# Group norm and attention over 16 images: the next image brought in as 16 pieces of four rows in place of 4 pieces of sixteen

## What is computed

```python
def _gn(v, G=32, eps=1e-5):
    ...
    m = jnp.mean(g, axis=(1, 2, 4), keepdims=True)
    s = jnp.var(g, axis=(1, 2, 4), keepdims=True)
    return ((g - m) / jnp.sqrt(s + eps)).reshape(v.shape)
...
qkv = jnp.einsum('bglc,dc->bgld', x, W_qkv) + b_qkv
score = jnp.einsum('bghlc,bghmc->bghlm', q, k) / scale
score = jax.nn.softmax(score, axis=-1)
out = jnp.einsum('bghlm,bghmc->bghlc', score, v)
...
x = x + _L0_conv_ref(_gn(x), L0_conv_W_qkv, L0_conv_b_qkv)
```

## Time and profile before

| what | value |
|---|---|
| median of 3 runs | 4365.6 us (4364.17 to 4367.62) |
| the profiled execution | 4368.04 us |
| its span in the profile | 4365.9 us |
| busy: PE, DVE, ACT, POOL | 3961.3, 3673.0, 3037.9, 1781.8 us |
| mean granted clock of PE | 0.963 of full speed |
| read from HBM, written | 134.42 MB, 134.22 MB |
| loads of images on ACT | 60 of 2048 KB, 9.6 us each to landing |
| DMA transposes on SP | 2048, 3.2 to 3.3 us each to landing |

### The profile page before, as it was taken

How to read it: one execution, slowest core, us unless ns; L and a number is a source line. 1 busy time by engine, 2 the same in 40 slices (tenths; PEclk the granted TensorE clock), 3 DMA queues, 4 the chain that set the end, 5 groups by cost and what they waited for, 6 DMA issues and landing times.

```text
span 4365.9 us, 144522 instructions
## 1 busy us (share of the span) xinstructions
PE 3961.3 (91%) x44133; PEld 3009.3 (69%) x44133; DVE 3673.0 (84%) x7138; ACT 3037.9 (70%) x8193; POOL 1781.8 (41%) x2065
## 2 busy tenths in 40 slices
PE   4898989989899898998989989899898988989998
PEld 3676767667676676766767667676676766767776
DVE  6896978879788797987979879798797987979987
ACT  3676767667676676766767667677676766767776
POOL 1443434434344343443434434344343433434444
PEclk9999999999999999999999999999999999999999
DMA  7999999999999999999999999999999999999999
GB/s 190 221 206 241 210 227 220 187 241 210 227 219 189 241 210 231 216 189 240 209 234 216 185 243 210 229 216 190 245 210 231 220 194 235 209 242 210 202 209 196
DMA packets 2508947, 944.11 MB, mean 216 GB/s; under 512 B 2180544, under 2 KB 2443072, under 8 KB 2508608
## 3 DMA queue, kind: packets, MB, share of 16 engines
q1 hardware_dynamic: 2384768, 814.22, 90.3%
q10 hardware_dynamic: 123840, 125.83, 9.1%
HBM read 134.42 MB, written 134.22 MB: 62 GB/s over the span
## 4 chain that ended last, share of the span: by engine, by line
PE 55%; DMA 13%; issue 12%; DVE 9%; SPq 7%; POOL 1%; ACT 1%; DVEq 1%; POOLq 0%; ACTq 0%
PE s_bank L297 15%; PE qk_bank L275 15%; PE o_bank L313 12%; DMA pt_hi<-p_hi 12%; PE v_bank L285 7%; PE xt_bank L267 4%; DVE neg_max L427 3%; SPq L227 3%; SPq L231 3%; PE v_bank L282 2%; DVE v_lo L440 1%; POOL p_hi L598 1%; DVE o_norm L453 1%; DVE bn L458 1%; DMA pt_lo<-p_lo 1%
## 5 line engine op out<-in xcount | busy, mean ns | idle before, releaser
L607 POOL TENSOR_TENSOR y_ring<-image,o_norm 128x256 f32<-128x256 f32 x1024 | 742.6, 725 | 2268.0 <-DVE o_norm L453 2268.0
L392 ACT ACTIVATE prob<-s_bank,neg_max 128x256 f32<-128x256 f32 x4096 | 1612.7, 492 | 69.8 <-issue 60.8
L373 ACT ACTIVATE qk<-qk_bank,b_in 128x256 f32<-128x256 f32 x2048 | 859.1, 471 | 950.8 <-PE qk_bank L275 949.5
L427 DVE TENSOR_REDUCE neg_max<-s_bank 128x2 f32<-128x512 f32 x2048 | 1313.2, 684 | 63.8 <-PE s_bank L297 62.8
L297 PE MATMUL s_bank<-qk 64*128 64x256 f32 x8192 | 1221.2, 418 | 45.5 <-issue 44.7
L434 DVE SCALAR_TENSOR_TENSOR p_lo<-prob,p_hi 128x1024 f16<-128x1024 f32 x1024 | 1239.5, 1210 | 4.9 <-POOL p_hi L598 1.4
L598 POOL TENSOR_SCALAR p_hi<-prob 128x1024 f16<-128x1024 f32 x1024 | 1068.6, 1044 | 312.4 <-DMA pt_hi<-p_hi 238.7
L275 PE MATMUL qk_bank<-xc,w_norm 128*128 128x256 f32 x4096 | 1190.1, 414 | 0.0
L313 PE MATMUL o_bank<-v_hi,pt_lo 128*128 128x65 f16 x8192 | 868.2, 195 | 282.0 <-DMA pt_hi<-p_hi 226.3
L275 PEld LDWEIGHTS qk_bank<-xc,w_norm 128*128 128x128 f32 x4096 | 714.1, 194 | 413.6 <-issue 342.9
L313 PEld LDWEIGHTS o_bank<-v_hi,pt_lo 128*128 128x128 f16 x8192 | 767.3, 99 | 304.1 <-DMA pt_hi<-p_hi 235.4
(11 more groups left out here) (71 smaller groups left out, 1922.8 us busy)
## 6 DMA issues: line engine op xcount, KB each, us to landing
x_ring<-image SPq DMA_DIRECT2D x512, 256.0 KB, 2.6
out_dram<-y_ring SPq DMA_DIRECT2D x512, 256.0 KB, 2.4
image<-in_x_dram ACTq DMA_DIRECT2D x60, 2048.0 KB, 9.6
pt_hi<-p_hi SPq DMA_TRANSPOSE x1024, 3.3
pt_lo<-p_lo SPq DMA_TRANSPOSE x1024, 3.2
image<-in_x_dram SPq DMA_DIRECT2D x4, 2048.0 KB, 16.5
w_in<-in_L_conv_W_qkv_dram SPq DMA_DIRECT2D x1, 192.0 KB, 2.4
b_in<-in_L_conv_b_qkv_dram SPq DMA_DIRECT2D x3, 0.5 KB, 2.1
```

The source lines that it names most:

```text
L373: ins = act.activation(qk[:, v % 2, t, :], qk_bank[:, t * TOK:(t + 1) * TOK], ACT.Identity, bias=b_in[:, t:t + 1])
L392: ins = act.activation(prob[:, m, c:c + TOK], s_bank[m][h][:, a * TOK:(a + 1) * TOK], ACT.Exp, bias=neg_max[:, m, h, a:a + 1])
L427: dve.tensor_reduce(neg_max[:, m, h, :], s_bank[m][h][:, :].rearrange("p (a k) -> p a k", a=J), AX.X, ALU.max, negate=True).then_inc(max_d ...
L607: pool.tensor_tensor(y_ring[:, m, :], image[:, par, bass.ds(row, 1), :].rearrange("p a c -> p (a c)"), o_norm[:, v % 2, :, :].rearrange("p ...
```

## The change

It has four parts. The next image but one is now brought in behind the image in work: in step r of image n, at every fourth step, ACT issues the load of four rows (r-20 to r-17) of image n+2 into the places of the same rows of image n, or, in steps 0 to 19, rows 44 to 63 of image n+1 into the places of image n-1. Each of the 15 images that are loaded so comes in 16 pieces of 512 KB, 240 loads in place of 60. The wait of each is for `y_done` to have passed the rows that it overwrites, 16 steps back. In image 0 the first 11 pieces of image 1 are issued within steps 0 to 7 with no wait. And the loop over images has 6 rounds in place of 7: images 13, 14 and 15 are written out, because the last two bring nothing or less.

```diff
-    LOADS = 4
...
-    SETTLE = UNROLL
-    assert SETTLE + LOADS * UNROLL <= STATS_FROM
+    LAG = STATS_FROM
+    CHUNKS = ROWS // UNROLL
...
+                if coming is not None and u == 0 and bring is not None:
+                    bring(base, *coming)
                 order(run, next_image)
...
                     for i in range(-2 * UNROLL, start):
-                        step(i // UNROLL * UNROLL, i // UNROLL * UNROLL, i % UNROLL, par, None,
-                             (LOAD, img + 1, 0) if i == UNROLL else None)
+                        if bring is not None and i >= 0:
+                            for c in range(i, CHUNKS - LAG // UNROLL, start):
+                                bring(None, 1, 1, c * UNROLL)
+                        step(i // UNROLL * UNROLL, i // UNROLL * UNROLL, i % UNROLL, par, None, None,
+                             (1, 1, ROWS - LAG + i) if i >= 0 else None)
...
                 with eng.Fori(0, GROUPS // UNROLL) as t:
                     for u in range(UNROLL):
                         step(t * UNROLL + g + STATS_FROM, t * UNROLL + STATS_FROM, u, par, None,
-                             None if last else (MEASURE, img + 1, t * UNROLL + u))
+                             None if last else (MEASURE, img + 1, t * UNROLL + u),
+                             None if final else (img + 2, par, t * UNROLL + (STATS_FROM - LAG)))
...
-            with eng.Fori(0, IMAGES // 2 - 1) as q:
+            with eng.Fori(0, IMAGES // 2 - 2) as q:
                 for s in range(2):
                     run_image(q * 2 + (1 + s), 1 - s, False, False)
-            run_image(IMAGES - 1, (IMAGES - 1) % 2, False, True)
+            for img in range(IMAGES - 3, IMAGES):
+                run_image(img, img % 2, False, img == IMAGES - 1)
...
-                if what[0] == LOAD:
-                    part = what[2]
-                    if not isinstance(what[1], int) or what[1] > 1:
-                        act.wait_ge(y_done, (what[1] - 1) * ROWS)
-                    rows = bass.ds(part * LB, LB)
-                    act.dma_start(image[:, 1 - par, rows, :], x_img[what[1], :, rows, :]).then_inc(loaded[1 - par], 16)
...
+            def bring(base, img, par, row, free=False):
+                if not (free or base is None or known_below(base, LAG)):
+                    act.wait_ge(y_done, base - (LAG - UNROLL))
+                rows = bass.ds(row, UNROLL)
+                act.dma_start(image[:, par, rows, :], x_img[img, :, rows, :]).then_inc(loaded[par], 16)
```

More of the change, by code:

```diff
@@ L37, in groupnorm_attention @@
     X_AHEAD = 2
-    MEASURE, LOAD = "measure", "load"
+    MEASURE = "measure"
     LOADS = 4
@@ L155, in wait_apart, with schedule, step @@
             eng.wait_ge(what, count).then_inc(waited, 1)
-        def schedule(eng, order, share=None):
-            def step(base, first_row, u, par, row=None, what=None):
+        def schedule(eng, order, share=None, bring=None):
+            def step(base, first_row, u, par, row=None, what=None, coming=None):
                 def run(lead, stage, *head):
@@ L172, in next_image @@
                         share(base, u, par, what, place)
+                if coming is not None and u == 0 and bring is not None:
+                    bring(base, *coming)
                 order(run, next_image)
             def run_image(img, par, first, last):
+                final = isinstance(img, int) and img + 2 >= IMAGES
                 g = img * ROWS
@@ L181, in run_image @@
                     for i in range(-2 * UNROLL, start):
-                        step(i // UNROLL * UNROLL, i // UNROLL * UNROLL, i % UNROLL, par, None,
-                             (LOAD, img + 1, 0) if i == UNROLL else None)
+                        if bring is not None and i >= 0:
[3 more added lines that the diff above has]
+                             (1, 1, ROWS - LAG + i) if i >= 0 else None)
                 else:
                     for i in range(SETTLE):
-                        step(g + i // UNROLL * UNROLL, 0, i % UNROLL, par, i)
+                        step(g + i // UNROLL * UNROLL, 0, i % UNROLL, par, i, None,
+                             None if last else (img + 1, 1 - par, ROWS - LAG + i))
                 with eng.Fori(0, (STATS_FROM - start) // UNROLL) as t:
                     for u in range(UNROLL):
-                        step(t * UNROLL + g + start, t * UNROLL + start, u, par, None,
-                             (LOAD, img + 1, t + (start - SETTLE) // UNROLL) if u == 0 and not last else None)
+                        step(t * UNROLL + g + start, t * UNROLL + start, u, par, None, None,
+                             None if last else (img + 1, 1 - par, t * UNROLL + (ROWS - LAG + start), first))
                 with eng.Fori(0, GROUPS // UNROLL) as t:
@@ L197, in run_image @@
                     step(g + row // UNROLL * UNROLL, 0, row % UNROLL, par, row,
-                         None if last else ("finish", img + 1, i))
+                         None if last else ("finish", img + 1, i), None if final else (img + 2, par, row - LAG))
                 if last:
@@ L399, in share @@
             def share(base, u, par, what, place):
-                if what[0] == LOAD:
-                    part = what[2]
-                    if not isinstance(what[1], int) or what[1] > 1:
-                        act.wait_ge(y_done, (what[1] - 1) * ROWS)
-                    rows = bass.ds(part * LB, LB)
-                    act.dma_start(image[:, 1 - par, rows, :], x_img[what[1], :, rows, :]).then_inc(loaded[1 - par], 16)
-                elif what[0] == "finish" and what[2] == FINISH - X_AHEAD:
+                if what[0] == "finish" and what[2] == FINISH - X_AHEAD:
                     act.wait_ge(stat_step, (what[1] + 1) * STAT_STEPS)
@@ L415, in order @@
                 run(0, v_high)
-            schedule(act, order, share)
+            def bring(base, img, par, row, free=False):
[3 more added lines that the diff above has]
+                act.dma_start(image[:, par, rows, :], x_img[img, :, rows, :]).then_inc(loaded[par], 16)
+            schedule(act, order, share, bring)
         @block.vector
@@ L563, in share @@
                     if u == 0:
-                        dve.wait_ge(loaded[1 - par], (what[1] - 1 + par) * (8 * LOADS)
-                                    + (1 - par) * (16 * LOADS))
+                        dve.wait_ge(loaded[1 - par], (what[1] - 1 + par) * (8 * CHUNKS)
+                                    + (1 - par) * (16 * CHUNKS))
                     measure(what[2], 1 - par)
```

## The result

| what | before | after |
|---|---|---|
| median | 4364.89 us (4 runs) | 4299.85 us (4 runs, 4288.51 to 4314.86) |
| ratio | | 0.9856, 95% interval 0.9821 to 0.9892 |
| span of the profiled execution | 4365.9 us | 4313.0 us |
| busy: PE, DVE, ACT | 3961.3, 3673.0, 3037.9 us | 3930.6, 3680.5, 3051.9 us |
| mean granted clock of PE | 0.963 | 0.975 |

The kernel became faster by 65 us, 1.4%. The forecast was 4151 us, 213 less than before; the range of 4060 to 4310 holds the result, near its upper end, and less than a third of the forecast gain came.

What follows compares the result with a forecast made beforehand. SP's issue pace was taken as the bound, with PE starved at loads. 4368.0 - 360 (loads) + 19.5 (start) + 136 (pieces) - 10 (loop return) = 4153.5 us profiled, 4151 us median; range 4060 to 4310.

Steps and rivals of the forecast that it cites:

- The bound: SP issues transposes without slack; four loads of sixteen rows delay it and starve PE, costing 24 us an image.
- What remains per piece: Cost of each 512 KB piece through SP's stretched transposes: 0.6 us, likely 0.4 to 0.9, 136 us for 227 pieces.
- the loop's return: Where the loop over images goes back, PE idles; six returns become five, saving 10 us.
- the 19.5 us for the start: In image 0 thirteen pieces come within eight steps, too close to win back, at 1.5 us each.
- It just fits, and the compute slips once: At `p_hi`, 1.6 us of slack covers a transpose landing 1.5 us late; otherwise compute slips a fraction once.
- Rival A: SP's pauses show whole, 1.5 us a piece, returning the loads' gain: 4356 us; chance 0.13 including nearby values.
- C: Rival: pause and ACT's issue ahead of the exponentials add up, 2.5 us a piece, about 4583 us; chance 0.05.
- D: Rival: each load's fixed DMA part shows, 288 us for the additional loads, 4644 us; chance 0.03.
- B: Rival: SP's stretch is absorbed too, 0 to 0.3 us a piece, 4015 to 4083 us; chance 0.13.
- E: Rival: ACT reaches its waits so late or early that pieces bunch up, leaving 4356 us; chance 0.02.
- The signs that I gave: Timeline signs of a right forecast: result spacing, even stretches, PE's clock, SP's stretch about 0.4 us, shorter POOL waits.
- A's sign: SP's transposes reaching 2.5 us beside each piece would show that the pauses count whole, 1.5 us a piece.

## Why the prediction was right and wrong

**The bound: right.** The loads were put at about 24 us an image, and through SP. With none from image 2 on 4033 us remain, 318 below the kernel with the old loads and the same loop (4350.86): 22.7 us for each of 14 images. SP as the engine without slack was named, and four experiments bear it out (no loads, one row, two rows, SP's wait left out).

**What remains per piece: wrong, and this is the step that failed.** I put it at 0.6 us, 0.4 for the issue of ACT beside SP's transpose and 0.2 for the queue filling up. Measured: 1.2 (267 us over 224 pieces), a size in the band of 1.1 to 1.5 that had got a chance of 0.13. The two parts were mis-sized in opposite ways. Over the whole span, summed as in the table, `pt_hi`, where the 0.40 had been seen, takes 1423 us to issue against 1378 with no loads, 0.2 us a piece, half of the 0.4. And `pt_lo`, the transpose behind it, takes 1497 against 1306, 0.85 us a piece, where I had 0.2; in the pair shown it is stretched by 1.16 and 1.20, of a pause of 1.5. The rest, up to 1.2, is in no transpose's issue. The reasoning behind the 0.2 was that a load of 6.7 us showed only 4.4 of stretch, so that 2.3 could stand outstanding. That subtraction treats a difference as a capacity. I take it that SP was also stopped for want of work around the load, with PE starved and `p_hi` late, and such time shows as no stretch; no run shows how much of the 2.3 that is. What the pieces show is that a pause of 1.5 us was not absorbed. With 1.2 in place of 0.6 the same sum gives 4368.0 - 360 + 19.5 + 227 x 1.2 - 10 - 2.4 = 4288 us; 4299.85 were measured. So the errors of the other terms add up to 12 us. Of them only the loop's return was measured by itself; of the 19.5 us for the start, POOL's first result shows 9.2, at 78.79 us where it was at 69.60.

**"It just fits, and the compute slips once": wrong.** I took the slack of 1.6 us at `p_hi` per piece, but it exists once: SP wins back 0.08 us in four steps, so what the first piece uses is missing for the next ones. And a slip is no small thing: the one shown costs 3.04 us of waiting and 1.6 of low clock, and the sum had no term for the clock. I had written that SP has no time to catch up, and did not carry it into the landing. DMA engines that are done before the next piece comes are no help where the issuing engine is the late one.

**Rival A, the bytes conserved,** had the size nearly right (1.5 us a piece) and 4356 us. Its reason, that the bytes are conserved, was wrong: with one row at a step the same bytes cost 110 us and not 267. That is 110 / 224 = 0.49 us for four rows: the one-row kernel, at 4142 us, does what I had forecast for the changed one. **C and D:** the issue ahead of the exponentials is covered, as costed at nothing (late issue: no gain); a load's fixed part does not show (0.05 us a small load). **B** is refuted by the 267 us, and **E** by ACT's timeline, whose two pieces stand 14.9 us apart. **The loop's return:** 8 us measured for 10.

The rule of the Trainium skill on the fixed cost of a DMA ("DMA: Bandwidth & Descriptors", section on the anatomy of a DMA, whose figures are a fit to DMAs that GpSimd issues, where ACT issues these) would have spoken for large pieces. Here, with nobody waiting for the landing, smaller ones were faster.

**The range** held the result only by the slice that it had for A: the forecast's own band ended at 1.1 us a piece and 4265 us.

**The signs that I gave.** Sixteen results in 62 us: 64.4. POOL's wait for `pt_hi` down to a few tens: 24.8. All stretches near 15.5 us per four steps: wrong, 16.55 on average. PE's clock at 1.00 in the first third of an image: 0.98 in image 7. No stretch above 0.4: wrong, `pt_lo` beside a piece takes 2.41 and 2.45 us in the pair shown and 2.02 on average in the steps counted above, against 1.24 with no loads; A's sign was 2.5.

## What to carry to other kernels

Look for the engine that can't win time back: where a queue's issues leave no gaps, every disturbance stays until someone else stalls, and slack of a buffer counts once and not per event. A bulk load in the background should come in pieces short enough that the issuing queue beside it is stretched little (here pieces of 0.75 us of the DMA engines cost less than half of what pieces of 1.5 did, for the same bytes), as small as their issue can be hidden; the number of loads cost next to nothing. Measure two sizes before choosing one. And when a stall is priced, look at the granted clock behind it: here it added half as much again.

## What the runs showed of the hardware that was not expected

- The DMA engines' own room didn't protect the issuing side: in the changed kernel 1.5 us in which 449 packets of a load passed and 15 of SP's queue stretched the issue of the transpose in progress from 1.25 to 2.41 us, though SP had just caught up.
- The answer to size is not a line: 128 KB a step cost 110 us in all, 256 KB at every second step 121, 512 KB at every fourth 267.
- A store put into ACT's queue behind a load of 2 MB landed 9.2 us after its issue, where one beside a load took 4.7 on SP: the kernel was 56 us slower, with 175.2 us of waits for the store. With pieces of 512 and of 128 KB the move stretched SP's transposes by 257 and 259 us in all.
- A wait of 3.04 us of PE was followed by a stretch at a granted clock of 0.66 (1790 to 1795), in which the scores of a row took 2.08 us in place of 1.14.
- Each return of the loop over images cost 8 to 11 us; the program with all 16 images written out had no wait of PE above 2.7 us behind image 0, and its length showed no price.
